# A shorter table of expert tiles, a re-timed selective scan and a layer norm moved to GpSimd, in an eight-phase kernel

## The reference

```
l0_ffn:  silu(x@w_gate * s_gate) * (x@w_up * s_up), then @ w_down * s_down   (int8 weights)
l1_attn: softmax(q k^T) v for 16 heads, then w_o; its result x is what the router reads
l1_ffn:  logits = x @ gate_w.T (32 experts); the 4 best of each token, softmax weights over them;
         a = silu(x@Wg[e]) * (x@Wu[e]), out = sum over the 4 of weight * (a @ Wd[e])
         plus a second, smaller set of experts of width 128 (16 of them), chosen by the same route
l2_attn: x, z = x @ in_proj; x = silu(conv4(x)); dt, B, C = x @ x_proj; delta = softplus(dt @ dt_proj + b)
         for t: h = exp(delta*A)*h + (delta*x)*B ; y_t = <h, C>          (512 channels x 16 states)
         out = ((y + x*D) * silu(z)) @ out_proj
```

## Time and profile before

| | |
|---|---|
| median of 3 runs | 2541.62 us (2540.76 to 2543.98) |
| the profiled execution | 2540.14 us; its span 2538.4 us; mean granted PE clock 0.936 of full |
| busy share of the span | PE 87%, PEld 76%, DVE 66%, ACT 57%, POOL 34% |
| l0_ffn | 241.5 to 368.5 us |
| l1_attn | 369 to 894 us |
| l1_ffn | 894.7 to 1204 us |
| l2_attn | 1205 to 1801 us |

### The profile page before, as it was taken

The page is one execution under the profiler, slowest core; times in us unless marked ns, Lnnn a source line. Parts: engine busy times, 40 slices in busy tenths (PEclk is TensorE's granted clock), DMA queues, the critical chain, the costliest instruction groups (busy, mean ns, idle before and its releaser), DMA issues. The chain is left out here.

```text
span 2538.4 us, 47638 instructions
## 1 busy us (share of the span) xinstructions
PE 2207.6 (87%) x16423; PEld 1931.7 (76%) x16423; DVE 1672.1 (66%) x4005; ACT 1449.6 (57%) x3812; POOL 864.6 (34%) x887
## 2 busy tenths in 40 slices
PE   6887979999999849999478988899696899996997
PEld 5776868999999839998256766677685576765997
DVE  5785868888888745552488887778364555554554
ACT  5775547777777613333477676776242666563442
POOL 3321110011111220000678787768486243422000
PEclk8998989999999969999689999999798999997999
DMA  4000110000000653332411111000400000000001
GB/s 150 1 1 17 49 53 18 2 18 18 18 18 18 207 141 115 119 103 88 135 41 49 51 51 47 34 34 1 119 1 1 1 1 1 1 1 1 1 1 34
DMA packets 74223, 111.77 MB, mean 44 GB/s; under 512 B 16026, under 2 KB 59666, under 8 KB 72868
## 3 DMA queue, kind: packets, MB, share of 16 engines
q1 hardware_dynamic: 66352, 87.22, 10.7%
q0 software_dynamic: 7488, 21.50, 2.6%
q10 hardware_dynamic: 148, 0.01, 0.0%
HBM read 79.73 MB, written 28.97 MB: 43 GB/s over the span
## 5 line engine op out<-in xcount | busy, mean ns | idle before, releaser
L1921 POOL TENSOR_TENSOR l2a_hb<-l2a_hb,l2a_Cb 128x1024 f32<-128x1024 f32 x128 | 303.1, 2379 | 117.3 <-DVE l2a_hb L2402 116.5
L2402 DVE TENSOR_TENSOR_SCAN l2a_hb<-l2a_dA,l2a_dB 128x1024 f32<-128x1024 f32 x128 | 289.2, 2275 | 72.0 <-PE l2a_dB L2008 27.4
L2243 ACT ACTIVATE l2a_dA<-l2a_delta,l2a_An 128x255 f32<-128x255 f32 x512 | 214.5, 498 | 26.3 <-DVE l2a_delta L2331 13.8
L2008 PE MATMUL l2a_dB<-l2a_diag,l2a_dxT 64*128 64x128 f32 x2048 | 187.8, 305 | 26.1 <-DVE l2a_hb L2402 13.3
L2008 PEld LDWEIGHTS l2a_dB<-l2a_diag,l2a_dxT 64*128 64x128 f32 x2048 | 138.9, 193 | 89.3 <-PE l2a_dB L2008 37.1
L964 PE MATMUL l1a_QK<-l1a_xh,early_wqkv_h 128*128 128x256 f32 x512 | 146.6, 286 | 1.5 <-DVE l1a_xl L128 1.5
L964 PE MATMUL l1a_QK<-l1a_xh,early_wqkv 128*128 128x256 f32 x512 | 144.1, 281 | 0.0
L964 PE MATMUL l1a_QK<-l1a_xl,early_wqkv_h 128*128 128x256 f32 x512 | 143.9, 281 | 0.0
L2028 PE MATMUL l2a_YS<-ident,l2a_hb 128*128 128x128 f32 x1024 | 140.4, 283 | 1.0 <-POOL l2a_hb L1921 1.0
L1223 ACT ACTIVATE l1a_ex<-l1a_S,l1a_nm 128x256 f32<-128x256 f32 x256 | 119.3, 471 | 36.7 <-DVE l1a_nm L1275 36.7
L2028 PEld LDWEIGHTS l2a_YS<-ident,l2a_hb 128*128 128x128 f32 x1024 | 115.1, 144 | 12.1 <-POOL l2a_hb L1921 1.2
(11 more groups left out here) (734 smaller groups left out, 7703.7 us busy)
## 6 DMA issues: line engine op xcount, KB each, us to landing
l2a_Cb<-c_rows SPq DMA_DIRECT2D x8, 2048.0 KB, 7.5
l1f_xl<-moe_x_rows SPq DMA_DIRECT2D x95, 128.0 KB, 2.0
moe_y_rows<-l1f_yo SPq DMA_DIRECT2D x95, 128.0 KB, 1.7
first_raw<-in_L_attn_w_qkv_dram SPq DMA_DIRECT2D x18, 256.0 KB, 2.8
moe_x_rows<-X SPq DMA_DIRECT2D x1, 4224.0 KB, 17.2
l1f_dL<-in_L_ffn_Wd_dram SPq DMA_DIRECT2D x1, 3072.0 KB, 16.9
X<-in_L_attn_x_dram SPq DMA_DIRECT2D x8, 256.0 KB, 6.0
routes_raw<-in_L_attn_w_o_dram SPq DMA_DIRECT2D x4, 512.0 KB, 4.2
```

The costliest lines, as they stand in the source:

```text
L1921: nc.gpsimd.tensor_tensor(h[:, :, :], h[:, :, :], Cb[p][:, s0:s0 + UN, :], ALU.mult).then_inc(hc_ready, 1)
L2008: last = nc.tensor.matmul(out[:, m:m + 2, j * P + a:j * P + a + HP], dxT[q][a:a + HP, j, c * P:(c + 1) * P], diag[q][a:a + HP, j, s0 + m:s ...
L2243: last = nc.scalar.activation(dA[(i * NU + u) % DAS][:, n, 1:SEQ], delta[q][:, c, 1:SEQ], ACT.Exp, scale=An[:, c, s0 + n:s0 + n + 1])
L2402: nc.vector.tensor_tensor_scan(flat(hb[u % RING]), flat(dA[(i * NU + u) % DAS]), dB[u % 2][:, :], 0.0, ALU.mult, ALU.add).then_inc(scanned, 1)
```

## The change

Three edits, independent of each other:

- **Norm of l0_ffn.** The two normalising instructions of each item leave VectorE and are done by GpSimd right behind its 1/std. VectorE waits for them (semaphore `x_normed`) before the statistics of the next item.
- **Table of tiles in two parts.** When item 7 is in l1_attn, the counts of items 0 to 5 are known, and they alone fill at least HEAD = 17 whole tiles. A table for these 17 is worked out in that item: two matmuls, 15 dependent steps of VectorE spread over steps 3 to 12, and a DRAM round trip by SP. l1_ffn starts from this table. Its table for the remaining tiles is worked out in the loop (8 steps on VectorE with tiles 0 to 3), stored by SP at t = 11, read back at t = 14 and waited for at t = 17. The routing weights (30 steps) go with tiles 4 to 18, the exponential of ACT with tile 5, the ternary pieces from tile 20 on. The four scatters at the end of l1_attn go to l1_ffn, with a semaphore of their own for the rows of items 6 and 7. SP loads the rows of 6 tiles first and then the 3 MB of down weights. `down` runs 4 tiles behind `gate_up` (it was 2), with 4 buffers `aT`.
- **Steps of l2_attn.** The z products of an item are done in its own steps 0 and 2, both through one PSUM bank (they were the next item's, in steps 0 and 1, in both banks). The chain that prepares the next item moves forward by one step or two on every engine, and dx on GpSimd from u = 12 to u = 10. The residual on VectorE moves from u = 7 to the end of u = 6, behind the MIX of that step.

The diff, cut to its core:

```diff
+            def normalize_here(k):
+
+                pool.wait_ge(ph.rstd_ready, k + 1)
+                for j in range(NT):
+                    nc.gpsimd.tensor_scalar(ph.X[:, k, j], ph.r[:, j, :], ph.mv[:, j, 0:1], ph.rstd[:, j:j + 1],
+                                            ALU.subtract, ALU.mult).then_inc(x_normed, 1)
...
+                    normalize_here(i - 2)
             rstd(ph, pool, ITEMS - 1)
+            normalize_here(ITEMS - 1)
...
-                dve.wait_ge(ph.x_done, k * 2 * NT + NT)
+                dve.wait_ge(ph.x_done, (k + 1) * NT)
+                dve.wait_ge(x_normed, k * NT)
                 add_and_stats(ph, dve, k, ys[:, :, :])
...
-                    if step == 7 and not first:
-                        normalize(ph, dve, i - 1)
...
+            sp.wait_ge(head_ready, 1)
+            sp.dma_start(routes.head_dram, routes.head_i[:, :]).then_inc(head_stored, 16)
+            sp.wait_ge(head_stored, 16)
+            for dst in (routes.head_row, routes.head_expert):
+                sp.dma_start(dst[:, :], routes.head_dram.rearrange("t c -> (t c)")[0:routes.HEAD * 4].rearrange("(a n) -> a n", a=1)
+                             ).then_inc(routes.head_loaded, 16)
             sp.wait_ge(qk_ready, ITEMS * NH)
...
                         scatter(nc, pool, sh, i - 2, j, qk_ready, i * NH + 9 + j * routes.TOPK)
-            pool.wait_ge(routing.idx_ready, ITEMS - 1)
-            scatter(nc, pool, sh, ITEMS - 2, 0)
...
+                    if step == 1 and i == ITEMS - 1:
+                        counts = YB[p][:, 2 * NT * routes.E:(2 * NT + 1) * routes.E]
+                        nc.tensor.matmul(counts, routes.ones[:, :], routes.run[:, 1, :], start=True, stop=False)
+                        nc.tensor.matmul(counts, routes.ones[:, :], routes.sel[:, 1, :], start=False, stop=True).then_inc(head_counted, 1)
...
+                    if 3 <= step < 3 + HEAD_OVER and i == ITEMS - 1:
+                        for n in range((step - 3) * HEAD_STEPS // HEAD_OVER, (step - 2) * HEAD_STEPS // HEAD_OVER):
+                            head_step(n, p)
...
+    XL, YO, AR, LAG = 6, 4, 4, 4
+    BACK = XL + LAG - 2
...
+            for t in range(TILES + BACK):
+                if t == XL:
+                    sp.dma_start(dL[:, :, :], w["L1_ffn_Wd"]).then_inc(down_loaded, 16)
+                if t == TAB_AT:
+                    sp.wait_ge(tab_ready, 1)
+                    sp.dma_start(tab_dram, tabi[:, :]).then_inc(tab_stored, 16)
+                if t == TAB_IN:
+                    sp.wait_ge(tab_stored, 16)
+                    for dst in (rowi, rowp):
+                        sp.dma_start(dst[:, :], tab_dram.rearrange("t c -> (t c)").rearrange("(a n) -> a n", a=1)).then_inc(tab_loaded, 16)
+                if t == HEAD:
+                    sp.wait_ge(tab_loaded, 32)
+                    sp.wait_ge(routes.late_rows_out, 16 * 2 * NT * TOPK)
...
+                if t + 1 == HEAD:
+                    pe.wait_ge(tab_loaded, 32)
...
-                if t >= 2:
-                    down(t - 2)
+                if t >= LAG:
+                    down(t - LAG)
...
+                    if q >= AR:
+                        dve.wait_ge(down_ready, q - AR + 1)
+                    nc.vector.tensor_copy(aT[q % AR][:, :, :].rearrange("p n t -> p (n t)"), AT[q % 2][:, 0:2 * P]).then_inc(aT_kept, 1)
+                if t < WEIGH_AT:
+                    tabulate(2 * t)
+                    tabulate(2 * t + 1)
+                elif t < WEIGH_AT + WEIGH // 2:
+                    weigh((t - WEIGH_AT) * 2)
+                    weigh((t - WEIGH_AT) * 2 + 1)
+                if t >= QUANT_AT:
+                    for n in range((t - QUANT_AT) * QC * QS // QUANT_OVER, (t - QUANT_AT + 1) * QC * QS // QUANT_OVER):
...
+                    if u == 7 and ahead:
+                        pool_diag(pool, i + 1, 1 - p, 0)
                     if u == 9 and ahead:
-                        pool_diag(pool, i + 1, 1 - p, 0)
+                        pool_diag(pool, i + 1, 1 - p, 1)
                     if u == 10 and ahead:
-                        pool_diag(pool, i + 1, 1 - p, 1)
-                    if u == 12 and ahead:
                         pool_dx(pool, i + 1, 1 - p)
...
-                    if u < 2 and ahead:
-                        pe_z(pe, k, q, u)
+                    if u in (0, 2):
+                        pe_z(pe, i, p, u // 2, ahead)
+                    if u == 3 and ahead:
+                        pe_low(pe, k)
+                    if u == 4 and ahead:
+                        pe_bc(pe, k)
                     if u in (3, 4) and not first:
-                        pe.wait_ge(z_kept, (i + 1) * NT + (NT if ahead else 0))
+                        pe.wait_ge(z_kept, (i + 1) * NT)
                         pe_turn_back(pe, i - 1, u - 3)
-                    if u == 3 and ahead:
-                        pe.wait_ge(z_kept, (i + 2) * NT)
-                        if ahead == 2:
-                            turn(ph, pe, i + 2, F[1])
-                    if u == 4 and ahead:
-                        if ahead == 2:
-                            pe.wait_ge(ph.xT_ready, i + 3)
-                        pe_low(pe, k)
                     if u == 5 and ahead:
-                        pe_bc(pe, k)
+                        pe_turn_b(pe, k)
                     if u in (5, 6) and not first:
                         pe_project(pe, i - 1, u - 5)
-                    if u == 7 and ahead:
-                        pe_turn_b(pe, k)
-                    if u == 8 and ahead:
+                    if u == 6 and ahead:
                         pe.wait_ge(b_kept, i + 2)
                         pe_dt(pe, k, 1)
-                        if not first:
+                    if u == 7 and ahead:
+                        if first:
+                            pe.wait_ge(z_kept, NT)
+                        else:
                             pe.wait_ge(ph.y_added, i)
                         pe_dt(pe, k, 0)
+                    if u == 12 and ahead == 2:
+                        pe_turn_x(pe, i)
+                    if u == 13 and ahead == 2:
+                        pe.wait_ge(ph.xT_ready, i + 3)
                     if u == 13 and ahead:
                         pe_dx(pe, k)
...
-                    if u == 7 and not first:
-                        residual(i - 1)
+                    if u == 8 and ahead:
+                        dve_plus(dve, i + 1, 1 - p)
                     if u == 10 and ahead:
-                        dve_plus(dve, i + 1, 1 - p)
-                    if u == 12 and ahead:
                         dve_delta(dve, i + 1, 1 - p)
                     if u in MIX and i + 3 < ITEMS:
                         dve_mix(dve, i + 3, *MIX[u])
+                    if u == 6 and not first:
+                        residual(i - 1)
```

407 lines of the change are left out of this document (258 added, 149 removed).

## The result

The changed kernel takes 2516.47 us (median of 4 runs, 2509.98 to 2519.88), the kernel before took 2541.19 beside it. The ratio estimated from all runs of both is 0.9897, 95% interval 0.9881 to 0.9913 (the two medians alone give 0.9903). It is faster by 24.7 us where 54 were forecast, and the time lies above the range's upper end of 2509. The profiled execution took 2519.74 us with a span of 2518.0, against 2538.4 before.

The account below looks back on a forecast made before the run. PE was taken as the bound, except for losses at l1_attn's barrier, l1_ffn's start and l2_attn's dx wait. Terms -2 + 0.7 - 28.4 - 24.7 = -54.4 took the median 2541.6 to 2487 us; 8 in 10 between 2464 and 2509.

Parts of the forecast that it names:

- l0_ffn, -2: In l0_ffn, moving the norm off VectorE removes a quarter of PE's 8.3 us of waits: -2 us.
- l1_attn, +0.7: In item 7 of l1_attn, the head table's 4.2 us on VectorE now and then makes PE late: +0.7 us.
- Barrier, -5.4: Behind l1_attn, with the scatters gone GpSimd's drain is 0.04 and the next phase starts sooner: -5.4 us.
- Start of l1_ffn, -23.0 from the phase's start: In l1_ffn, the early table brings gate_up forward, PE waiting some 4 us for down weights: -23.0 us.
- l2_attn, -24.7: In l2_attn, dx comes earlier and PE's 5.36 us wait goes, -3.8 in each of items 1 to 4: -24.7 us.
- the term of +3: In item 7 of l2_attn, the item does its two z products itself, 1.88 each: +3 us.
- VectorE's cluster at u = 6: In l2_attn, scan, MIX pair, statistics and residual take 7.7 us on VectorE against a step's 4.2; PE idles 5.0.
- The first (the hole in l2_attn only moves, -4 to -8 there): In l2_attn, VectorE's cluster delays the low-rank delta as much as dx gains: time about 2506 us, chance 0.20.
- the table's rival: In l1_ffn, down weights land 8 us later and VectorE sets the pace: -19 for -28.4, 2496 us, chance 0.09.
- above 2510 would mean that the start of l1_ffn is not bound as I worked it out: Sign to check: a kernel time above 2510 us would put the miss at the start of l1_ffn.
- Slower by the clock: In l2_attn, two idle places an item bring PE's clock down: +56 for -24.7, 2568 us, chance 0.03.
- GpSimd blocking `al`: In l0_ffn, VectorE's subtraction waits out a GpSimd instruction: +2 for -2, 2491 us, chance 0.3.

Follow-up runs that it names:

- e2: Kernel before with only the norm of l0_ffn moved to GpSimd: 2537.72 us, ratio 0.9975.
- e3: Kernel before with only the new steps of l2_attn: 2527.66 us, ratio 0.9940.
- e8: Changed kernel with the four scatters of item 6's first tile back at the end of l1_attn: 2512.13 us, ratio 0.9875.
- e11: Changed kernel with the scatters of items 0 and 1 issued twice, 64 indirect DMAs for 48: GpSimd's drain 6.07 us; no kernel time given.
- e1: Changed kernel run again, nothing edited: 2512.54 us, ratio 0.9881.
- e16: Changed kernel with the 3 MB load of down weights in four parts, down(0) waiting for the first; second group of runs: 2500.97 us, ratio 0.9831.
- e15: Changed kernel once more, unedited, in a later group of runs: 2513.00 us, ratio 0.9886.
- e6: Changed kernel with `plus`, ln, delta and dx of l2_attn each one step later: 2513.37 us, ratio 0.9876.
- e9: Changed kernel with l2_attn's residual at step 7 for 6, and plus, ln, delta and dx one step later: 2506.38 us, ratio 0.9851.
- e4: Kernel before with only the two-part table of tiles (l1_attn and l1_ffn): 2523.56 us, ratio 0.9926.
- e5: Changed kernel with the second half of the small down weights loaded in l1_ffn, ahead of the 3 MB load: 2519.21 us, ratio 0.9905.
- e13: Changed kernel with the 3 MB load of down weights in four parts, down(0) waiting for the first; first group of runs: 2510.11 us, ratio 0.9869.
- e12: Changed kernel with down products six tiles late for four, and the 3 MB load behind row load 7 for 5: 2510.60 us, ratio 0.9869.
- e18: Changed kernel with l2_attn's residual at step 7, plus, ln, delta, dx a step later, load whole; second group of runs: 2510.23 us, ratio 0.9864.
- e10: Changed kernel with the 16 scatters of l1_ffn waiting until the 3 MB load has landed: 2508.48 us, ratio 0.9859.
- e7: Changed kernel with the 3 MB load of down weights issued first in l1_ffn, on ScalarE's queue: 2519.89 us, ratio 0.9903.

## Why the prediction was wrong

The sign was right and the size was twice too large. Three of its steps failed: the barrier's drain, the wait for the down weights, and the items of l2_attn. Step by step:

- **l0_ffn, -2.** The number is right, -2.2, but by luck: half of the waits went and not a quarter (those for `al`, 4.0), and the end of the stage cost +1.7, more than its bound of +1.3, as each of GpSimd's two instructions takes 1.2 us there.
- **l1_attn, +0.7.** Right for item 7 (62.50 to 63.26, +0.76 over its neighbours). A step there lasts 62.2 / 16 = 3.9 us and not the 4.2 that I took, so the free time is 6.0 and not 6.5, still more than the 4.2 added. Not foreseen: items 1 to 6 went from 62.23 to 62.50 each in every kernel with the table, and not in e2 and e3. The order of instructions there is the same; most products of the projections take 280 to 282 ns in the mean where they took 278 to 279. That is 1.6 us over six items. The cause wasn't looked for by a run and stays open.
- **Barrier, -5.4.** Measured -2.3. The failed step is "With the scatters gone the drain is 0.04": it is 4.77. The reading behind it, that the drain waited for four scatters to land, is right for 2.0 of its 7.1 us (e8); the rest is 0.85 and 82 ns for every indirect DMA of the phase (e11), and 48 of them remain. The rows that I compared with, x8 of 40 ns, are another drain of each barrier, not GpSimd's first one, which takes 0.8 us even with no indirect DMA.
- **Start of l1_ffn, -23.0 from the phase's start.** Measured -20.3 (e1) and -17.9. gate_up(0) at 6.9 for 7.2 and gate_up(4) at 17.5 for 18.6 are right. The failed step is "PE waits some 4 us there, does down(0)": it is 7.8 us, and PE does not stand in front of down(0) but for the rows of tile 6. I counted the six row loads ahead of the 3 MB and not the ones behind it on the same queue; with the load asked for at 8.4 for 6.9 and landing in 17.3 for 16.9, gate_up(5) came at 29.6 for 26.2. e16 shows that the hole was this one load in one piece: with it in parts, 2.9 us lie between gate_up(4) and (5). The other 2.4 us of the first execution go with the late completions, which nothing in the profile before could show.
- **l2_attn, -24.7.** Measured -9.5 and -8.4, and -12.3 in e15: the largest miss. By items, in the first execution:

| | item 0 | items 1 to 4 | item 5 | item 6 | item 7 | outside them |
|---|---|---|---|---|---|---|
| forecast | -4 | -15.2 | -5 | -3.5 | +3 | 0 |
| measured | -5.9 | -11.0 | -1.2 | +0.5 | +6.2 | +1.9 |

The failed step is "Items 5 and 6 have no MIX: -5 and -3.5", which carried the 5.36 us wait of one middle item to items that don't have it. PE's waits of item 5 in the kernel before were:

```profile
PE l2a_T L1991 <- POOL l2a_t L1858: 2.3, 1, 2.3
PE l2a_dB L2008 <- DVE l2a_hb L2402: 1.2, 1, 1.2
PE l2a_T L2037 <- ACT l2a_t L2191: 0.4, 1, 0.4
```

They add to 3.9. The new order has 4.0 there, 3.6 of it for VectorE's scan, so nothing was gained: PE stands idle for 65.80 - 60.51 = 5.3 us before and 64.60 - 59.12 = 5.5 after. In item 7 the term of +3 was too small: PE's own work there grew by 5.05 us (45.98 for 40.93, at a clock of 0.96 for 1.00) and its idle time by 1.15. The second failed step is the cause named for what remains, VectorE's cluster at u = 6 with the MIX pair in it. The changed kernel has the same wait of PE, 3.2 us, in items 5 and 6 without MIX and in item 2 with it. In item 2:

```profile
1416.33 0.69 DVE L135 TENSOR_TENSOR l2a_r<-X,l2a_T 128x512 f32<-128x512 f32 x1 [0.72 <-PE l2a_T L2193]
...
1424.17 0.70 DVE L2464 SCALAR_TENSOR_TENSOR l2a_T<-l2a_t,l2a_T 128x512 f32<-128x512 f32 x1 [1.72 <-ACT l2a_t L2319]
...
1428.90 2.17 PE L2158 MATMUL l2a_dB<-l2a_diag,l2a_dxT 64*128 64x128 f32 x16 [3.23 <-DVE l2a_hb L2551]
```

VectorE has caught up at u = 6, where it waits 0.72 for PE; it is late at `plus`, where it stands 1.72 for ScalarE's parts. e6 and e9 moved these places and the period moved by 0.3 to 0.5 only. That fits a delay which the three engines hand round, with no single step of VectorE as the bound; it is argued from these two edits, and what bounds the period stays open.
- **Rivals.** The first (the hole in l2_attn only moves, -4 to -8 there) is nearest in its stage; that it and a part of the table's rival held together, and the barrier with them, is the case that the range left out. I had put them side by side, and not summed. Of the mark "above 2510 would mean that the start of l1_ffn is not bound as I worked it out" the runs say: true, but of the 34 us between the two spans (-54.4 and -20.4) this stage holds 5.1, l2_attn 15.2, the barrier with l1_attn 4.8 and stages that nobody touched 9.0 (7 of which were absent in e1's execution). Part of l2_attn's 15.2, some 3 us by the table under e1 to e4, is the lower clock at its start.
- **Slower by the clock, GpSimd blocking `al`.** Neither: the clock rose to 0.97 in the items, and `al` keeps its 416 ns. The rule of the Trainium skill ("SBUF — State Buffer", section "Who interferes with whom"), that GpSimd blocks a VectorE instruction with two SBUF inputs, is not seen in `al`'s median here; only two more of the 64 are long, 0.56 and 0.68. What grows beside it is GpSimd's own instruction, also where it had begun first.

Open: the late completions at l1_ffn's start. They are in the first execution, in all kernels of the group e5 to e8 and in all of e13 to e15, and in none of e1 to e4, e9 to e12 and e16 to e18; the same code and the same chip have both. With them 650 to 920 of some 17,900 semaphore records are missing from the trace. Nothing that was edited turned them on or off, and whether they are the chip's or come with the recording isn't known. The Trainium skill ("NOTIFIC — the notification-queue block", section 7.1 on overflow) describes both a mode in which records are dropped when their ring is full and one in which the engine that writes them is stalled; no run here shows whether either is at work. With the load whole and where the changed kernel has it, the stage took 290.6 to 294.5 with them (the changed kernel, e6, e8, e15) and 289.3 to 292.0 without (e1, e4, e9, e10, e11, e18), so in the mean they cost some 2 us, though the two ranges overlap, and they can hide what an edit does at this place, as in e13.

## What to carry to other kernels

A large load that several consumers need piece by piece should be cut, with its first piece and the small loads that are needed before the rest issued in turn: here 9 to 10 us came from the order of the same bytes (in the runs without late completions; 3 and within the noise in those with them), about as much as all the hand-moved steps of l2_attn gave. When a wait is measured in one item of a loop, read it in every kind of item before multiplying, and look what stands behind a big DMA on its queue, not only ahead. Gains of several parts that are all "a little less idle, a bit more clock" did not add here, 44 us apart and 32 together; forecast the sum below the sum of the parts, and let the range hold two of the rivals at once. Before a few us of a stage are put down to an edit, compare the clock at which the stage began.

## What the runs showed of the hardware

- GpSimd's drain at the end of a phase took 82 ns more for each scatter that was added to the phase, though the 16 added ones had landed over 200 us before: 4.77 us with 48, 6.07 with 64 (e11). Some 0.8 is there with none; four scatters just issued add another 2.0 (e8).
- A tensor-scalar instruction of 128x256 on GpSimd took 1.22 us with VectorE idle and up to 2.11 beside a busy VectorE, where the copy of 128x512 takes 0.61 at the least. VectorE's subtraction with two inputs in SBUF kept its 0.42 us beside it, with two exceptions in 64.
- While 3 MB were on their way, the three row loads of 128 KB issued behind them on the same queue took 17.4 to 17.7 us to land, and 2.1 otherwise (e1). With the 3 MB on another engine's queue, and issued first, the first row load took 16.6 (e7).
- The same unedited start of l2_attn ran at a mean clock of 0.61 or of 0.67, and the stage took 2 to 4 us more at the lower one (e1 and e15, one kernel, 592.8 and 588.9). What decides between them is open.
- The same products in l1_attn took 1 to 3 ns more in each of hundreds of instructions in every kernel with the head table; the cause is open.
